# Two groups' mixes in one PSUM bank, heads interleaved by 16 rows, with new orders of work

## The reference

```
x  = x + attention16(layernorm(x))            # 16 heads of width 8, no mask       (ATTN0)
x  = x + relu(layernorm(x) @ w1 + b1) @ w2 + b2
z  = x + attention16_rope_causal(layernorm(x)) @ wo                                # ATTN1
y  = layernorm(z)
for l in 0, 1:                                # 8 heads of width 64, window 64     (LOCAL0, LOCAL1)
    y = y + local_attention(rotary(l2norm(q)), rotary(l2norm(k)), v) @ wo2[l]
    y = y + geglu(layernorm(shift(y)) * g + b) @ w2_2[l] + b2_2[l]                 # (FEED0, FEED1)
out = x + y
```

## Time and profile before

| what | value |
|---|---|
| median of 3 runs | 2964.49 us (2964.08 to 2968.03) |
| profiled execution: time | 2968.08 us |
| profiled execution: span | 2966.4 us |
| instructions | 69962 |
| mean granted TensorE clock | 0.982 |
| DMA | 22.72 MB, mean 8 GB/s |

### The profile page before, as it was taken

The page is one execution under the profiler, slowest core; times in us unless marked ns, Lnnn a source line. Parts: engine busy times, 40 slices in busy tenths (PEclk is TensorE's granted clock), DMA queues, the critical chain, the costliest instruction groups (busy, mean ns, idle before and its releaser), DMA issues.

```text
span 2966.4 us, 69962 instructions
## 1 busy us (share of the span) xinstructions
PE 2714.0 (91%) x24680; PEld 1949.3 (66%) x24680; DVE 2337.2 (79%) x5888; ACT 2126.4 (72%) x5956; POOL 1606.6 (54%) x1747
## 2 busy tenths in 40 slices
PE   5778999999999999999999999999999999999887
PEld 3445666666666676666667666666766666676665
DVE  3467778888888888888888888888888888887764
ACT  2356687777778777877877777787777778777663
POOL 1035455565555556555655655565565556556653
PEclk8889999999999999999999999999999999999999
DMA  2000000000000000000000000000000000000000
GB/s 80 3 3 4 5 4 7 5 6 7 7 7 4 7 5 6 7 7 7 5 6 5 6 7 7 7 5 6 5 7 6 7 7 5 6 7 5 5 3 8
DMA packets 41990, 22.72 MB, mean 8 GB/s; under 512 B 21130, under 2 KB 40884, under 8 KB 41652
## 3 DMA queue, kind: packets, MB, share of 16 engines
q1 hardware_dynamic: 41652, 18.24, 2.2%
HBM read 9.86 MB, written 4.19 MB: 5 GB/s over the span
## 4 chain that ended last, share of the span: by engine, by line
PE 53%; ACT 25%; DVE 16%; issue 3%; POOL 2%; DMA 0%; SPq 0%; DVEq 0%; POOLq 0%; ACTq 0%
PE bank L1175 8%; DVE negmax L900 7%; PE bank L1075 6%; ACT P L792 5%; ACT probs L760 5%; PE bank L1247 4%; PE bank L1186 4%; PE bank L1140 3%; PE bank L1255 3%; ACT rawP L792 3%; PE bank L1239 3%; PE bank L1031 3%; PE bank L1212 3%; PE bank L1096 2%; PE bank L1206 2%
## 5 line engine op out<-in xcount | busy, mean ns | idle before, releaser
L760 ACT ACTIVATE probs<-bank 128x512 f32<-128x512 f32 (+1 forms) x1024 | 478.1, 568 | 206.2 <-PE bank L1119 205.4
L900 DVE TENSOR_REDUCE negmax<-bank 128x2 f32<-128x512 f32 (+1 forms) x896 | 555.1, 683 | 54.4 <-PE bank L1096 40.5
L1175 PE MATMUL bank<-wqkv_sb,hS 128*128 128x512 f32 x768 | 399.8, 623 | 23.2 <-ACT rawA L797 12.4
L692 POOL TENSOR_TENSOR rn<-ss_kept,minus_half 128x16 f32<-128x16 f32 x128 | 372.7, 2912 | 64.8 <-DVE ss_kept L960 64.8
L637 POOL TENSOR_TENSOR veps<-moments,eps_tile 128x2 f32<-128x2 f32 x192 | 38.9, 203 | 641.9 <-DVE moments L852 640.8
L659 POOL TENSOR_SCALAR_AFFINE_SELECT probs<-probs 128x256 f32<-128x256 f32 x512 | 200.2, 413 | 234.8 <-ACT probs L760 234.5
L1140 PE MATMUL bank<-probs,V 128*16 128x256 f32 (+1 forms) x4096 | 246.7, 359 | 25.1 <-POOL probs L659 18.4
L680 POOL TENSOR_TENSOR rawA<-rawA,rope_sb 128x512 f32<-128x512 f32 x128 | 186.3, 1456 | 90.4 <-ACT rawA L779 90.3
L980 DVE TENSOR_REDUCE negmax<-bank 128x2 f32<-128x384 f32 (+1 forms) x384 | 207.1, 595 | 35.0 <-PE bank L1212 34.8
L680 POOL TENSOR_TENSOR rawB<-rawB,rope_sb 128x512 f32<-128x512 f32 x128 | 177.7, 1388 | 85.5 <-ACT rawB L779 85.3
L792 ACT ACTIVATE P<-bank,negmax 128x192 f32<-128x192 f32 x512 | 208.4, 453 | 5.2 <-DVE negmax L980 3.4
(11 more groups left out here) (140 smaller groups left out, 7293.7 us busy)
## 6 DMA issues: line engine op xcount, KB each, us to landing
xin<-x SPq DMA_DIRECT2D x32, 128.0 KB, 2.1
out<-xout SPq DMA_DIRECT2D x32, 128.0 KB, 1.8
feed_h<-YB SPq DMA_DIRECT2D x64, 63.5 KB
wqkv_sb<-wqkv SPq DMA_DIRECT2D x1, 1536.0 KB
feed_h<-YB SPq DMA_DIRECT2D x64, 0.2 KB
rawQ<-c_masks SPq DMA_DIRECT2D x1, 832.0 KB
w_sb<-w SPq DMA_DIRECT2D x1, 682.0 KB
w_sb<-w SPq DMA_DIRECT2D x2, 256.0 KB, 2.9
```

The costliest lines, as they stand in the source:

```text
L692: nc.gpsimd.tensor_tensor(rn[:, l, t].rearrange("p m h -> p (m h)"), ss_kept[:, l, t].rearrange("p m h -> p (m h)"), minus_half[:], ALU.po ...
L760: nc.scalar.activation(dst, src, ACT.Exp, scale=SCALE0 if k == ATTN0 else SCALE1)\
L900: nc.vector.reduce_max(negmax[:, k, t, head:head + 4 * many - 3:4], tile(u, e)[:, :].rearrange("p (h k) -> p h k", h=many), AX.X, negate=T ...
L1175: mm(tile(u)[:], hS[:, l, t * P:(t + 1) * P], wqkv2_sb[:, l, m * INNER:(m + 1) * INNER], start=True, stop=True).then_inc(has_filled(u), 1)
```

## The change

**Layout of V.** V gets 544 columns a key tile: two halves of 272, each with eight heads of 32 columns (8 values, a one, 23 zeros), and 16 columns of zeros at the end of each half. The weight of head 4g+n is always the 32 columns from 32(4g+n) on. In groups 0 and 1 these are [values, one, zeros | 16 zeros]. In groups 2 and 3 the half's offset of 272 shifts them: [16 zeros | values, one, zeros]. So a product of head h fills rows 32n to 32n+15, one of head h+8 rows 32n+16 to 32n+31, and both add zeros to the other's rows.

**Mixes.** Groups g and g+2 now accumulate into the same bank: the first group starts it, the second stops it. Only the second raises `full`, and DVE copies once for both, so two copies an attention in place of four. The units run in the order of groups 0, 2, 1, 3. Each bank is held from the first group's mix to the copy behind the second's. The number of mix products is the same; their weights have 32 columns in place of 16.

**Attention's end.** `oT` has two pieces a key tile in place of four, so `attn_out` has two transposes in place of four, writes 256 columns, and DVE reads it with heads 16 apart in the order 0, 8, 1, 9, ...; reciprocal and product are of the same size.

**Orders and tables.** All order strings and bank tables are new. There are 27 rounds; the fill and the drain hold five sequences (419 + 376 = 795 units on PE). Of identity products there are 7 a round: 4 ahead of ATTN0's `maxes` 1 and 3 ahead of LOCAL0's `shift`. Over the whole kernel they are 340 in place of 488: 60 in place of 134 in the part before the rounds, 189 in place of 286 in the rounds, 91 in place of 68 behind them.

```diff
-ROUNDS = 26
+ROUNDS = 27
...
 TURNS = {
     "tensor": (
-        "3333002222200001210102222101201123333311003033333331330113113002222111113333330031133303444422232222"
-        "22221111301401244022222220422132300003305555505550250001233"
+        "2413500123503305050222330533003303202232110500020102322201120310144243113333330303313110351153102023"
+        "33222331311100153123232332234011211301021224242240022202222"
...
-STEADY_FILLERS = {(ATTN0, "scores", 1): (3, 0), (ATTN0, "maxes", 1): (3, 1), (ATTN1, "scores", 0): (3, 0), (LOCAL0, "qkv2", 0): (2, 0)}
+STEADY_FILLERS = {(ATTN0, "maxes", 1): (4, 3), (LOCAL0, "shift", 0): (3, 0)}
 END_FILLERS = {
-    (0, ATTN0): {("turn_q", 0): 5, ("mix", 0): 7, ("mix", 1): 7, ("mix", 2): 7, ("mix", 3): 7, ("turn", 0): 8},
-    (1, ATTN0): {("turn_q", 0): 5, ("mix", 0): 7, ("mix", 1): 3, ("mix", 2): 7, ("turn", 0): 8},
-    (31, LOCAL1): {("qkv2", 2): 9, ("turn_p", 0): 10},
-    (31, FEED1): {("turn", 0): 28},
+    (0, ATTN0): {("mix", 0): 7, ("mix", 1): 6},
+    (1, ATTN0): {("maxes", 2): 5, ("mix", 0): 4},
+    (0, ATTN1): {("mix", 1): 5},
+    (2, ATTN0): {("mix", 0): 4},
+    (30, LOCAL0): {("shift", 0): 6, ("qkv2", 0): 4, ("scores2", 1): 5},
+    (31, LOCAL0): {("shift", 0): 6, ("qkv2", 0): 4},
+    (30, LOCAL1): {("turn_p", 0): 15},
+    (31, LOCAL1): {("turn_q2", 0): 19},
+    (31, FEED1): {("turn", 0): 27, ("down2", 0): 5},
 }
 NBANKS = 8
 
@@ -234,9 +227,9 @@
         return Unit("scores", g, bank=4, **(dict(masked=4) if rotary else {}))
 
     def mix(g):
-        return Unit("mix", g, bank=1)
-
-    for g in range(GROUPS):
+        return Unit("mix", g, bank=1 if g < GROUPS // 2 else 0)
+
+    for g in (0, 2, 1, 3):
         units += [scores(g), mix(g)]
     units += [Unit("attn_out", t, bank=1, rec_done=1) for t in range(TT)]
     return units
@@ -401,13 +394,15 @@
         KB = sb("KB", [P, 2, TT, H16, 32])
         qT = sb("qT", [P, 2, GROUPS, SEQ], f32r)
         kT = sb("kT", [P, 2, GROUPS, SEQ], f32r)
-        V = sb("V", [P, 2, TT, H16, 16])
+        V = sb("V", [P, 2, TT, 2 * 272])
+        V_heads = V[:, :, :, :].rearrange("p k t (a c) -> p k t a c", a=2)[:, :, :, :, 0:256].rearrange(
+            "p k t a (i c) -> p k t a i c", c=32)
         rawC = sb("rawC", [P, 2, 1024])
         probs_in = sb("probs", [P, 3 * 1024 + 512])
 
         probs = [probs_in[:, 0:2048].rearrange("p (t j q) -> p t j q", t=TT, j=4),
                  probs_in[:, 2048:3584].rearrange("p (j q) -> p j q", j=4)]
-        oT = rawC[:, :, :].rearrange("p a (g q) -> p a g q", g=GROUPS)
+        oT = rawC[:, :, 0:512].rearrange("p a (g q) -> p a g q", g=GROUPS // 2)
         up0T = rawC[:, ATTN0, :].rearrange("p (c q) -> p c q", c=FF0 // P)
         cosine1 = rawC[:, ATTN1, 0:512].rearrange("p (t n) -> p t n", t=TT)
         sine1 = rawC[:, ATTN1, 512:1024].rearrange("p (t n) -> p t n", t=TT)
@@ -598,7 +593,7 @@
             sp.wait_ge(stored, 16 * BATCH + 16)
 
         ALL_LOADED = [16 * n for n in N_LOADS]
-        PRESETS = [7, 15]
+        PRESETS = [8, 17]
         CLEARED = NBANKS
 
         @block.gpsimd
@@ -607,12 +602,13 @@
             nc.gpsimd.memset(eps_tile[:], EPS).then_inc(setup_pool, 1)
 
             def preset(k):
-                so_many = PRESETS[k] - 5
+                so_many = PRESETS[k] - 6
                 nc.gpsimd.memset(QB[:, k], 0.0).then_inc(setup_pool, 1)
                 nc.gpsimd.memset(KB[:, k], 0.0).then_inc(setup_pool, 1)
                 nc.gpsimd.memset(V[:, k], 0.0).then_inc(setup_pool, 1)
                 pool.wait_ge(setup_pool, so_many + 3)
-                nc.gpsimd.memset(V[:, k, :, :, HD8:HD8 + 1], 1.0).then_inc(setup_pool, 1)
+                for t in range(TT):
+                    nc.gpsimd.memset(V_heads[:, k, t, :, :, HD8:HD8 + 1], 1.0).then_inc(setup_pool, 1)
                 nc.gpsimd.memset(KB[:, k, :, :, 24:26], 1.0).then_inc(setup_pool, 1)
 
             preset(ATTN0)
@@ -732,8 +728,8 @@
                     t = u.part
                     src = tile(u)
                     act.wait_ge(has_filled(u), uses(u))
-                    nc.scalar.activation(V[:, k, t, :, 0:HD8], src[:, 2 * DIM:3 * DIM].rearrange("p (h d) -> p h d", h=H16),
-                                         ACT.Copy).then_inc(sig("v_ready", u), 1)
+                    nc.scalar.activation(V_heads[:, k, t, :, :, 0:HD8], src[:, 2 * DIM:3 * DIM].rearrange(
+                        "p (a i d) -> p a i d", a=2, d=HD8), ACT.Copy).then_inc(sig("v_ready", u), 1)
                     qk = src[:, 0:2 * DIM]
                     if k == ATTN1:
                         act.wait_ge(sig("rot_done", u), so_far("rot_done", u) + 1)
@@ -909,9 +905,10 @@
                     dve.wait_ge(sig("m_hi", u), so_far("m_hi", u) + 1)
                     nc.vector.tensor_tensor(place[:, :, 25].bitcast(f32r), neg, place[:, :, 24], ALU.subtract)\
                         .then_inc(sig("m_ready", u), 1)
-                elif u.kind == "mix":
-                    dve.wait_ge(has_filled(u), uses(u))
-                    nc.vector.tensor_copy(oT[:, k, u.part, :], tile(u)[:, 0:SEQ]).then_inc(has_emptied(u), 1)
+                elif u.kind == "mix" and u.part >= GROUPS // 2:
+                    both = earlier(u, "mix", u.part - GROUPS // 2)
+                    dve.wait_ge(has_filled(both), uses(both))
+                    nc.vector.tensor_copy(oT[:, k, both.part, :], tile(both)[:, 0:SEQ]).then_inc(has_emptied(both), 1)
                 elif u.kind == "mix2":
                     dve.wait_ge(has_filled(u), uses(u))
                     nc.vector.tensor_copy(o2T[:, l, 2 * u.part:2 * u.part + 2, :].rearrange("p c q -> p (c q)"), tile(u)[:])\
@@ -919,11 +916,13 @@
                 elif u.kind == "attn_out":
                     t = u.part
                     dve.wait_ge(has_filled(u), uses(u))
-                    heads = tile(u)[:, :].rearrange("p (h c) -> p h c", c=32)
+                    heads = tile(u)[:, 0:SEQ].rearrange("p (h c) -> p h c", c=16)
                     nc.vector.reciprocal(recip[:, k, t, :], heads[:, :, HD8]).then_inc(sig("rec_done", u), 1)
                     dve.wait_ge(sig("rec_done", u), so_far("rec_done", u) + 1)
-                    nc.vector.tensor_tensor(att[k][:, t, :].rearrange("p (h d) -> p h d", h=H16), heads[:, :, 0:HD8],
-                                            recip[:, k, t, :].unsqueeze(2).broadcast_to([P, H16, HD8]), ALU.mult)\
+                    nc.vector.tensor_tensor(att[k][:, t, :].rearrange("p (a i d) -> p i a d", a=2, d=HD8),
+                                            heads[:, :, 0:HD8].rearrange("p (i a) d -> p i a d", a=2),
+                                            recip[:, k, t, :].rearrange("p (i a) -> p i a", a=2).unsqueeze(3)
+                                            .broadcast_to([P, H16 // 2, 2, HD8]), ALU.mult)\
                         .then_inc(has_emptied(u), 1)
                 elif u.kind == "residual":
                     for sem, count in newest(*(taken(earlier(u, "attn_out", t)) for t in range(TT))):
@@ -1133,17 +1132,20 @@
                     else:
                         src = earlier(u, "scores", g)
                         pe.wait_ge(sig("masked", src), so_far("masked", src) + 4)
+                    both = earlier(u, "mix", g - GROUPS // 2) if g >= GROUPS // 2 else u
                     for t in range(TT):
                         q0 = P if k == ATTN1 and t == 1 else 0
                         for n in range(4):
                             part = probs[k][:, t, n, :] if k == ATTN0 else probs[k][:, n, t * SEQ:t * SEQ + SEQ - q0]
-                            last = mm(tile(u)[32 * n:32 * n + 16, q0:SEQ], V[:, k, t, 4 * g + n, :], part, start=t == 0, stop=t == 1)
-                    last.then_inc(has_filled(u), 1)
+                            last = mm(tile(both)[32 * n:32 * n + 32, q0:SEQ], V[:, k, t, 32 * (4 * g + n):32 * (4 * g + n) + 32], part,
+                                      start=both is u and t == 0, stop=both is not u and t == 1, skip_group_check=True)
+                    if both is not u:
+                        last.then_inc(has_filled(both), 1)
                 elif u.kind == "attn_out":
                     t = u.part
-                    for sem, count in newest(*of("mix", *range(GROUPS)), free(u)):
-                        pe.wait_ge(sem, count)
-                    for g in range(GROUPS):
+                    for sem, count in newest(*of("mix", *range(GROUPS // 2)), free(u)):
+                        pe.wait_ge(sem, count)
+                    for g in range(GROUPS // 2):
                         last = turn(tile(u)[:, g * P:(g + 1) * P], oT[:, k, g, t * P:(t + 1) * P], ident)
                     last.then_inc(has_filled(u), 1)
                 elif u.kind == "project1":
```

138 lines of the change are left out of this document (63 added, 75 removed).

## The result

The changed kernel takes 2949.37 us (median, 2945.92 to 2951.99), the kernel before 2964.47 us. The ratio is 0.9946, with a 95% interval of 0.9928 to 0.9963: 0.5% faster, 15 us where 64 were forecast and where the range ended at 2945.

What follows compares the result with a forecast made beforehand. PE was taken to bound a round; 28.2 us for transposes and 35.6 for identity products made 63.8, bringing the span from 2966.4 to 2902.6 us and the forecast to 2901 us, with a range of 2852 to 2945 us.

Steps and rivals of the forecast that it cites:

- What bounds the kernel: In a round, PE is the bound: busy 82.2 of 86.3 us, with 7.7 us of slack in filler and pauses.
- Fewer identity products: In PE's rounds, 4 of 11 go at 0.33 us each: 1.32 us a round, 36 us in 27 rounds.
- I take the upper end: For the rounds' identity products, the full 1.32 us a round was counted, from bounds of 0 and 1.32.
- rival 1: In the rounds, pauses stay open and fillers' time turns idle; only the transposes count: 2936 us, chance 0.17.
- Fewer transposes: At the attentions' end, 8 of 16 a round go: 0.88 us a round, 28 us over 32 sequences; bounds 0.5 and 1.1.
- The new order: In PE's list, the cycle of a round stays nearly the old one, with swaps of a place or two.
- sum of pauses: PE's pauses in a round stay at 4.1 us, with bounds of 2 us less and 2 us more.
- the tight place: At ATTN0's last group, between scores and mix, a new pause of 0.4 to 0.9 us.
- Wider weights: In the mixes, 128 loads a round grow by 14 ns each, hidden behind running matmuls: nothing; 1.8 us a round if exposed.
- DVE, ACT, POOL: Beside PE, four DVE copies a round go, 1.7 us of 72.5, costed at nothing; ACT's table loads and POOL also nothing.
- Banks: Mix banks held until the second group is through, 5 to 10 more bank-us of 691 a round: costed at nothing.
- Rival 5: In the fill and drain, the clock falls with fewer identity products, costing at most 33 us: 2934 us, chance 0.05.

Runs made afterwards that it cites:

- new_turns4: The changed kernel with each transpose at the attentions' end done twice, 16 a round in place of 8: 2975.32 us, ratio 1.0037.
- new_fill11: The changed kernel with 4 identity products a round put back, ahead of LOCAL0's first projection and ATTN1's first maxima: 2968.98 us, ratio 1.0009.
- old_turns2: The kernel before with 8 transposes a round fewer, leaving half of the heads out of the result: 2951.86 us, ratio 0.9950.
- new_half_project: The changed kernel with the local attentions' output projections over two of their four pieces only: 2935.11 us, ratio 0.9900.
- new_one_table: The changed kernel with Relu for Gelu on ACT, so it never changes table between Gelu and Exp: 2935.15 us, ratio 0.9903.
- old_wide: The kernel before with mix weights of 32 columns, 16 more of them zeros, each group still in its own bank: 2974.89 us, ratio 1.0039.
- old_turns2_copies2: old_turns2 with DVE's copies of groups 2 and 3 cut to one column in place of 256: 2955.08 us, ratio 0.9958.
- new_banks: The changed kernel with only its bank table written anew, each use getting the bank that came free first: 2975.98 us, ratio 1.0032.
- new_no_fill: The changed kernel without the 7 identity products of its rounds: 2964.31 us, ratio 1.0007 to the kernel before.

## Why the prediction was wrong, step by step

**What bounds the kernel: half right.** PE is the busiest engine in a round, but the page's chain of 53% PE and 25% ACT should have been read as the bound itself. The round is a closed chain over PE, ACT, DVE and POOL with near ties: PE work that was put on it cost all of its time in one place (new_turns4, 0.87 us for 8 transposes) and half in another (new_fill11), work that is taken from it pays until the next path is the longest, 0.3 to 0.5 us later (old_turns2, new_half_project, new_one_table).

**Fewer identity products: the step that failed.** "I take the upper end" was wrong: 1.32 us a round, 36 us in all, measured at 0.0. The round at the full clock is 85.7 us with 7 products or with none, and in the kernel before 86.3 with 11 and 86.4 with none. The products stood where PE waits anyway, as the rows of `maxes` 1 show. The prediction had both bounds and the right reason for the lower one, "at a real pause their removal leaves idle time in their place", and rival 1 was this case, down to its sign, PE idle of 5 us or more (5.3). Rival 1's 2936 us was still 13 too low, since it counted the transposes in full. The sum of idle and filler time shows the same: 3.6 + 4.1 = 7.7 us before, 2.2 + 5.3 = 7.5 after.

**Fewer transposes: the right work, mis-sized gain.** PE's time for them fell by 0.11 us each as counted. On the round they are worth 0.5 us and not 0.88 (old_turns2: 86.3 to 85.8), some 15 us over the kernel in place of 28. The prediction's own lower bound was 0.5, with a lengthened pause as its reason; that the rest is lost to a next path fits the other runs and isn't traced. In the ends, where 4 us were counted, nothing came in the change. In old_turns2's execution the ends are 6.2 us shorter and keep their clock, so the change may have gained there and lost it to its lower clock; one execution of each doesn't settle it.

**The new order: sum of pauses wrong, the tight place right.** The pauses rose by 1.2 us a round, not by 0. The order isn't shown to cost or bring time by itself: with the old order the saved transposes give 85.8 to 85.9, the changed kernel has 85.7. What it brings is that the merge can be had at all: under the old order it took 87.7 us a round or more at the full clock, and mostly 88.8.

**Wider weights: hidden in the rounds, open elsewhere.** The load takes 110 ns as worked out from 96 and 138, and the rounds don't change (old_wide). old_wide as a whole is 11 us slower, 4.6 of them in the fill of its profiled execution, which the prediction left out and no run explains. The rule of the Trainium skill ("TensorE: Matmul & The Clock Gate", The mechanism), that a load overlaps running matmuls only in another row group, doesn't hold for these rounds: by it 1.8 us a round would have been paid, and old_wide's took 86.3 to 86.4 where before took 86.3. The prediction cited one half of it: the same section of the Trainium skill also lets a load that goes to the background weight buffer be pulled ahead of running matmuls, and that fits these rounds. The Trainium skill, same page, section LDWEIGHTS, has a load last its columns divided by 1.2 ns, 13 ns for 16 columns more. The trace's difference of 14 agrees; the whole load of 32 columns, 109 ns, is far above the 27 by that formula, and the measurement decides.

**DVE, ACT, POOL: right for the copies.** Cutting them changes no round (old_turns2_copies2). But ACT isn't free: 2.6 us less of its work gives 0.3 us a round (new_one_table).

**Banks: right for the change, with its own table.** No wait on a mix's copy shows in the rounds of the changed kernel. But costed at nothing they are a term of some 26 us: that is what another table takes (new_banks). The 5 to 10 bank-us that the prediction adds for the held banks are 0 to 12 by its own terms (four of 4 to 7 for eight of 2); nothing hangs on it.

**The clock: half seen.** Rival 5 looked for it in the ends, where it moved (0.86 for 0.88, 0.95 for 0.97) and cost some 3 us by the medians of the two runs with more products there, 6.4 by one execution. It was left out where it mattered more: the identity products of the rounds hold the full clock there, and their full removal cost 56 us in the kernel before and 15 in the changed one.

With the two terms as measured, 0.5 us a round for the transposes and 0.0 for the identity products, the sum would have been 27 to 32 x 0.5 = 14 to 16 us, or 2948 to 2951 us.

## What to carry to other kernels

Where one engine is 95% busy in a steady round and the chain passes through others for half of it, a term of work on that engine is worth between nothing and all of its time: filler that stands in pauses is worth nothing, and real work pays only until the next path is the longest. Adding a known piece of work tells whether it is on the path, removing one tells how far away the next path is; both are needed, since they gave 0.87 and 0.5 us here. Judge filler by the clock that it holds and by where it runs, ahead of a wait or behind it, and not by the time that it takes. And when a trace's chain passes over a piece, look at what would stand in its place: four identity products lay on the chain for 1.19 us and cost nothing.

## What the runs showed of the hardware

A round without identity products (new_no_fill) ran in 85.7 us at a granted clock of 1.00 and in 87.8 us when its mean was 0.96. By that mean about 7 us of the round ran at 1.2 GHz (an estimate: 0.04 x 2 x 87.8). They cost 2.1 us of the round and 3.0 of PE's busy time (81.4 for 78.4), although PE is idle for 7.3 us of the same round at the full clock.

Weight loads of 32 columns took 109 ns where those of 16 took 95, and 128 of them a round, 1.8 us in sum, lengthened no round (old_wide).
